# An adaLN block with linear attention and a routed softmax layer: the row statistics of the second modulated norm split over VectorE, ScalarE and GpSimd

## The chip, the cores and the metric
The kernel runs on 1 core of one Trainium2 chip. The metric is the device time of one execution in microseconds.

## The reference, cut to what matters
For each of 4 batches of 2048 rows with 256 elements the block computes:

```
h = layernorm(x) * (1 + ca) + sa
x = x + ga * favor_attention(h)              # linear attention, 16 heads
h = layernorm(x) * (1 + cb) + sb             # second modulation
x = x + gb * ffn(h)
ffn(h): for each of 4 experts (512 rows each)
    xn = (h - mean(h)) * rsqrt(var(h) + 1e-5) * norm_w + norm_b     # second statistics
    q, k, v = projections of the first 256 >> e elements of xn
  softmax attention over all 2048 rows, 8 heads
  out = projection + h
```

Every row of the second half thus needs two sets of statistics: those of x for the modulation, and those of the modulated row h for the norm inside the ffn. The change touches both.

## The kernel before, in words
The four batches run one after the other, each in three parts. The first part works over 16 tiles of 128 rows (linear attention features and sums). The last part is a long loop over 60 slots of score, exponential and value products (lines 1103, 1522, 893, 1695, 1707 and 1720). Between them lies a transition of some 80 us, and all edits are in it.

The transition goes over 4 slots s of 512 rows (one expert each, in the order 3, 1, 0, 2), each in two halves h of two 128-row tiles; I write (s, h). No planner decides anything: each engine has a list of calls written out by hand, and waits on semaphores. For one (s, h) the work is:

- TensorE: `projected` (L1571) puts out the attention output, `second_transposes` (L1580), `second_values` (L1590) and `second_qk` (L1600).
- VectorE: `residual` (L1146) adds to X; `statistics_of_x` (two L996, two L1000, one L1006) puts variance + eps in VE; `modulated` (two L1157, two L1161) makes Hh; `statistics_of_h` (two L996, two L1000, L1005, L1006) puts minus the mean in NEGM and variance + eps in VE; `merged` (L1139), `reciprocals` and `low_part` (L1171) serve other steps. `low_part` puts the low half of a q or k block in QKS.
- GpSimd: `deviations` (L564) takes VE to the power -0.5 for the modulation; `deviations_again` (L569, L571) does the same for the second statistics, and multiplies NEGM by it into NMR.
- ScalarE: `centred` (L773) makes X2 from Hh with scale RSTD and bias NMR; `normal` (L785), `second_values` (L791) and `high_part` (L802, the high half into QKS) empty TensorE's banks.
- SyncE: one in-order queue stores each block of QKS to q_scr or k_scr (L399) and, at the end of a slot, waits for the slot's stores and then loads operands for the last part (L378, L396, L410). Block n of q or k uses buffer n % 3 of QKS, so `high_part` of block n waits for the store of block n - 3. The blocks are 0 to 2 (slot 0), 3 to 5 (slot 1), 6 to 9 (slot 2) and 10 to 12 (slot 3).

GpSimd's calls for slot 2 stand in the order `deviations(2, 0)`, `deviations(2, 1)`, `deviations_again(2, 0)`, `deviations_again(2, 1)`.

## Time and profile before

| | us |
|---|---|
| median of 3 runs | 1781.54 |
| lowest and highest | 1776.65, 1785.52 |
| the profiled execution | 1779.44 |
| its span | 1777.6 |
| TensorE busy | 1692.4 (95%) |
| VectorE busy | 1381.0 (78%) |
| ScalarE busy | 1085.2 (61%) |
| GpSimd busy | 1123.3 (63%) |

The profiled execution took 1779.44 us, 1.8 us more than its span. Busy shares are means over parts with different limits; the transition is read by itself below. A matmul's end is modelled in the trace, so its start and the wait before it say more than its end. The granted clock of TensorE has a mean of 0.972 of full speed.

### The profile page before, as it was taken

The page shows a single profiled execution, that of the slowest core. Times are in us where ns is not written, and L with a number is a line of the kernel's source. Part 1 is how long each engine was busy: PE and PEld are TensorE (multiplying, and loading weights), DVE is VectorE, ACT ScalarE, POOL GpSimd, SP SyncE. Part 2 cuts the span into 40 slices and gives each one's busy share as a digit, 9 for nine tenths or more (in the row PEclk, how much of TensorE's full clock was granted, in tenths as well). Part 3 has the DMA queues.
Part 4 walks back from the last instruction along what each step waited for, and adds up shares of the span by engine and source line. Part 5 has one row for each costly group of instructions (what it writes and reads, how often), then busy time and mean ns, then how long its engine had stood idle before and what let it go on. Part 6 is the DMA issues. An engine that isn't in the chain of part 4 may idle for free.

```text
span 1777.6 us, 31990 instructions
## 1 busy us (share of the span) xinstructions
PE 1692.4 (95%) x11538; PEld 972.0 (55%) x11538; DVE 1381.0 (78%) x2629; ACT 1085.2 (61%) x2066; POOL 1123.3 (63%) x1058
## 2 busy tenths in 40 slices
PE   6999989999999989999999998999999999899998
PEld 4775544444577554444467755444437765444443
DVE  5987977776588788787678878877848878778783
ACT  1885536666688543666668844466667875356664
POOL 2784358677678344876767734686776862477774
PEclk8999989999999999999999999999999999899999
DMA  5000360010200045001110005400120001620201
GB/s 187 2 1 2 111 178 15 19 46 24 73 1 2 1 151 143 10 19 46 57 40 2 1 14 176 105 19 10 46 72 25 2 1 51 187 64 12 50 5 48
DMA packets 56077, 89.57 MB, mean 50 GB/s; under 512 B 13288, under 2 KB 31976, under 8 KB 53100
## 3 DMA queue, kind: packets, MB, share of 16 engines
q1 hardware_dynamic: 54768, 87.45, 17.0%
q8 instruction: 93, 1.52, 0.4%
q14 instruction: 64, 0.52, 0.1%
q10 hardware_dynamic: 1152, 0.07, 0.0%
HBM read 49.29 MB, written 35.72 MB: 48 GB/s over the span
## 4 chain that ended last, share of the span: by engine, by line
PE 69%; DVE 16%; ACT 8%; DMA 2%; issue 2%; SPq 2%; POOL 1%; ACTq 0%; DVEq 0%; POOLq 0%
PE PS L1695 14%; PE PS L1522 13%; PE PS L1707 12%; PE PS L1720 7%; PE PS L1416 5%; DVE MXP L1103 4%; PE PS L1441 3%; PE PS L1424 3%; PE PS L1451 3%; ACT HT L662 2%; ACT HTR L665 2%; DVE STAT L996 2%; DVE QKS L1171 1%; ACT PHIQ L703 1%; PE PS L1571 1%
## 5 line engine op out<-in xcount | busy, mean ns | idle before, releaser
L623 POOL TENSOR_TENSOR TS<-PR 128x1024 f32<-128x1024 f32 (+1 forms) x248 | 551.3, 2236 | 273.6 <-ACT PR L893 208.8
L1103 DVE TENSOR_REDUCE MXP<-PS 128x1 f32<-128x512 f32 x960 | 588.8, 681 | 145.2 <-PE PS L1522 144.6
L893 ACT ACTIVATE PR<-PS 128x512 f32<-128x512 f32 x960 | 487.5, 624 | 302.0 <-PE PS L1695 282.4
L1522 PE MATMUL PS<-KOP,QOP 96*128 96x512 f32 x960 | 406.2, 436 | 9.6 <-DVE MXP L1103 3.3
L1695 PE MATMUL PS<-QOP,KOP 97*128 97x512 f32 x960 | 389.7, 429 | 8.8 <-ACT PR L893 5.7
L1522 PEld LDWEIGHTS PS<-KOP,QOP 96*128 96x128 f32 x960 | 186.2, 195 | 168.9 <-issue 89.6
L1695 PEld LDWEIGHTS PS<-QOP,KOP 97*128 97x128 f32 x960 | 179.9, 189 | 153.1 <-ACT PR L893 130.1
L1707 PE MATMUL PS<-PR,V 128*32 128x512 f32 x1920 | 256.1, 607 | 0.0
L1707 PEld LDWEIGHTS PS<-PR,V 128*32 128x32 f32 x1920 | 65.8, 113 | 150.2 <-issue 110.8
L1720 PE MATMUL PS<-TS,ones 128*32 128x512 f32 x960 | 139.2, 618 | 0.0
L541 POOL TENSOR_SCALAR PK<-XSK 128x1024 f32<-128x1024 f32 x64 | 67.1, 1048 | 102.2 <-ACT XSK L725 102.2
L1451 PE MATMUL PS<-PB,QKT 64*128 64x256 f32 x1536 | 125.5, 296 | 1.0 <-DVE VE L990 1.0
L1451 PEld LDWEIGHTS PS<-PB,QKT 64*128 64x128 f32 x1536 | 99.3, 186 | 36.9 <-issue 25.4
L1416 PE MATMUL PS<-W1T,HTR 128*128 128x512 f32 x384 | 107.3, 415 | 2.7 <-POOL HTR L485 2.6
L501 POOL TENSOR_TENSOR SQ<-SQ 128x256 f32<-128x256 f32 (+2 forms) x192 | 96.1, 501 | 17.9 <-ACT SQ L682 3.1
L1043 DVE TENSOR_REDUCE MXQ<-PS 128x16 f32<-128x1024 f32 x64 | 78.3, 1223 | 21.2 <-PE PS L1451 21.1
L1441 PE MATMUL PS<-ident,XSQ 128*128 128x128 f32 x512 | 84.4, 292 | 9.5 <-ACT PHIQ L703 9.5
L494 POOL TENSOR_SCALAR XH<-X,MV,RSTD 128x256 f32<-128x256 f32 x64 | 78.4, 1225 | 11.0 <-POOL RSTD L478 10.4
L1053 DVE TENSOR_TENSOR XSK<-PS,MXK 128x1024 f32<-128x1024 f32 x64 | 78.4, 1225 | 7.1 <-DVE MXK L1049 0.9
L1043 DVE TENSOR_REDUCE MXK<-PS 128x16 f32<-128x1024 f32 x64 | 78.4, 1225 | 6.9 <-PE PS L1451 2.7
L703 ACT ACTIVATE PHIQ<-PS 128x512 f32<-128x512 f32 x128 | 76.3, 596 | 10.7 <-PE PS L1441 10.7
L564 POOL TENSOR_TENSOR RSTD<-VE,minus_half 128x2 f32<-128x2 f32 x32 | 22.9, 714 | 93.2 <-DVE VE L1006 93.2
(157 smaller groups left out, 2559.4 us busy)
## 6 DMA issues: line engine op xcount, KB each, us to landing
KOP<-k_scr SPq DMA_DIRECT2D x84, 256.0 KB, 5.6
k_scr<-QKS SPq DMA_DIRECT2D x64, 256.0 KB, 2.9
QOP<-q_scr SPq DMA_DIRECT2D x180, 64.0 KB, 2.0
q_scr<-QKS SPq DMA_DIRECT2D x40, 256.0 KB, 2.9
X<-in_L_attn_x_dram SPq DMA_DIRECT2D x16, 512.0 KB, 3.9
out_dram<-X SPq DMA_DIRECT2D x12, 512.0 KB, 2.9
QOP<-MXT SPq DMA_DIRECT2D x224, 0.5 KB
KOP<-QKS SPq DMA_DIRECT2D x36, 64.0 KB, 2.0
```

The lines of the kernel that those rows point to most:

```text
L501: g.tensor_tensor(sq[:, :, 0:w], sq[:, :, 0:w], sq[:, :, w:2 * w], ALU.add).then_inc(S["n2_half"], 1)
L623: g.tensor_tensor(sums(k)[:, 0:len(stage)], pair[:, :, 0], pair[:, :, 1], ALU.add).then_inc(S["psum_t"], 1)
L893: a.activation(PR[:, k % 2, w, q], bank(score_bank(p, n, w, q)), ACT.Exp).then_inc(S["ex"], 1)
L1043: return mark(v.tensor_reduce(mx[:], heads(src), AX.X, ALU.max))
L1103: v.tensor_reduce(MXP[:, u % 2, i, kc:kc + 1], bank(max_bank(p)), AX.X, ALU.max).then_inc(S["am_rd"], 1)
L1416: last = mm(bank(4), HTR[:, x_, k], W1T[:, w_, k], start=m == 0 and k == 0, stop=m == len(PARTS) - 1 and k == KD - 1)
L1441: last = tr(bank(at_bank)[:, q * P:(q + 1) * P], XSQ[:, t % 2, (half * 4 + q) * P:(half * 4 + q + 1) * P], ident[:])
L1451: last = mm(bank(base + r)[:, 2 * P * j:2 * P * (j + 1)], QKT[rows, x_, 2 * j + o], PB[rows, w_, j, 2 * P * r:2 * P * (r + 1)], start=m == ...
L1522: mm(bank(max_bank(p)), QOP[0:96, u % QS6, i * P:(i + 1) * P], KOP[0:96, h % KS6, kc * CH:(kc + 1) * CH], start=True, stop=True).then_inc( ...
L1695: mm(bank(score_bank(p, n, w, q)), KOP[:, units[u][0] % KS6, kt * P:(kt + 1) * P], QOP[:, u % QS6], start=True, stop=True).then_inc(S["sc_ ...
L1707: last = mm(PS[r:r + DH, 6, :], V2[:, 2 * n + q, h * DH:(h + 1) * DH], PR[:, k % 2, w, q], start=n == 0, stop=n == STEPS - 1, tile_positio ...
L1720: last = mm(PS[r:r + DH, 7, :], ones[:], sums(2 * m + q)[:, w], start=n == 0, stop=n == STEPS - 2, tile_position=(0, r))
```

## The change
The addition of eps to the variance of x moves from VectorE to GpSimd (`statistics` ends with L1000). `modulated`'s second instruction also puts out the row sum of h into NEGM (`accum_out`). GpSimd's new `means` scales that sum to minus the mean. ScalarE's new `squared` computes (h - mean)^2 for two tiles with the row sum into VE, and GpSimd's `deviations_again` scales that and adds eps before the power. `statistics_of_h` is gone from VectorE's list. The orders on ScalarE and GpSimd get the new calls.

```diff
                 def deviations(s, h):
-                    wait_all(pool, (S["ve2"], n))
+                    wait_all(pool, (S["ve2"], 2 * n))
+                    g.tensor_scalar(VE[:, cols], MV[:, cols, 1], NORM_EPS, None, ALU.add).then_inc(S["ve2_e"], 1)
+                    wait_all(pool, (S["ve2_e"], n))
                     g.tensor_tensor(RSTD[:, cols], VE[:, cols], minus_half[:, cols], ALU.pow).then_inc(S["rstd2"], 1)
+
+                def means(s, h):
+                    wait_all(pool, (S["h2"], 2 * n))
+                    g.tensor_scalar(NEGM[:, cols], NEGM[:, cols], -1.0 / D, None, ALU.mult).then_inc(S["negm"], 1)

                 def deviations_again(s, h):
                     wait_all(pool, (S["ve3"], 2 * n))
+                    g.tensor_scalar(VE[:, cols], VE[:, cols], 1.0 / D, NORM_EPS, ALU.mult, ALU.add
+                                    ).then_inc(S["ve3_e"], 1)
+                    wait_all(pool, (S["ve3_e"], n))
                     g.tensor_tensor(RSTD[:, cols], VE[:, cols], minus_half[:, cols], ALU.pow).then_inc(S["rs3"], 1)
-                    wait_all(pool, (S["rs3"], n))
+                    wait_all(pool, (S["rs3"], n), (S["negm"], n))
                     g.tensor_tensor(NMR[:, cols], NEGM[:, cols], RSTD[:, cols], ALU.mult).then_inc(S["nmr3"], 1)
...
                 deviations(2, 0)
+                means(2, 0)
+                deviations_again(2, 0)
                 deviations(2, 1)
-                deviations_again(2, 0)
+                means(2, 1)
                 deviations_again(2, 1)
...
+                def squared(s, h):
+                    act.wait_ge(S["negm"], 2 * (NC * b + s) + h + 1)
+                    for i in (2 * h, 2 * h + 1):
+                        t = s * TPC + i
+                        a.activation(XSQ[:, h, (i - 2 * h) * D:(i - 2 * h + 1) * D], Hh[:, t], ACT.Square,
+                                     bias=NEGM[:, t:t + 1], accum_out=VE[:, t:t + 1]).then_inc(S["ve3"], 1)
...
                 for t in tiles:
-                    v.bn_aggr(MV[:, t], STAT[:, t]).then_inc(S["dve_own"], 1)
-                    own.n += 1
-                dve.wait_ge(S["dve_own"], own.base + own.n)
-                sl = slice(tiles[0], tiles[-1] + 1)
-                if negated:
-                    v.tensor_scalar(NEGM[:, sl], MV[:, sl, 0], -1.0, None, ALU.mult).then_inc(S[signal], 1)
-                v.tensor_scalar(VE[:, sl], MV[:, sl, 1], NORM_EPS, None, ALU.add).then_inc(S[signal], 1)
+                    v.bn_aggr(MV[:, t], STAT[:, t]).then_inc(S[signal], 1)
...
                         v.scalar_tensor_tensor(Hh[:, t], Hh[:, t], RSTD[:, t:t + 1], MODB[:, b, 1, :], ALU.mult,
-                                               ALU.add).then_inc(S["h2"], 1)
-
-                def statistics_of_h(s, h):
-                    dve.wait_ge(S["h2"], TPC * (NC * b + s) + 2 * h + 2)
-                    statistics(halves(s, h), [Hh[:, t] for t in halves(s, h)], "ve3", negated=True)
+                                               ALU.add, accum_out=NEGM[:, t:t + 1]).then_inc(S["h2"], 1)
```

For the other slots GpSimd's list gets `means(s, h)` right ahead of `deviations_again(s, h)`. On ScalarE `squared(0, 0)` stands ahead of `centred(0, 0)`, `squared(0, 1)` behind it, `squared(1, 0)` ahead of `high_part(0, 0)`, `squared(1, 1)` ahead of `high_part(0, 1)`, `squared(2, 0)` ahead of `high_part(1, 0)`, `squared(2, 1)` ahead of `high_part(1, 1)`, `squared(3, 0)` ahead of `high_part(2, 0)` and `squared(3, 1)` ahead of `high_part(2, 3)`.

GpSimd's list for slot 2 in the kernel before (L564 is `deviations`, L569 and L571 `deviations_again`):

```order
L564 TENSOR_TENSOR RSTD<-VE,minus_half 128x2 [waits ve2] x2
L569 TENSOR_TENSOR RSTD<-VE,minus_half 128x2 [waits ve3]
L571 TENSOR_TENSOR NMR<-NEGM,RSTD 128x2 [waits rs3]
L569 TENSOR_TENSOR RSTD<-VE,minus_half 128x2 [waits ve3]
L571 TENSOR_TENSOR NMR<-NEGM,RSTD 128x2 [waits rs3]
```

The same place in the changed kernel, from `deviations(2, 0)` to `deviations(2, 1)` (L564 and L566 are `deviations` there, L571 is `means`, L576, L579 and L581 are `deviations_again`):

```order
L564 TENSOR_SCALAR VE<-MV 128x2 [waits ve2]
L566 TENSOR_TENSOR RSTD<-VE,minus_half 128x2 [waits ve2_e]
L571 TENSOR_SCALAR NEGM<-NEGM 128x2 [waits h2]
L576 TENSOR_SCALAR VE<-VE 128x2 [waits ve3]
L579 TENSOR_TENSOR RSTD<-VE,minus_half 128x2 [waits ve3_e]
L581 TENSOR_TENSOR NMR<-NEGM,RSTD 128x2 [waits negm,rs3]
L564 TENSOR_SCALAR VE<-MV 128x2 [waits ve2]
L566 TENSOR_TENSOR RSTD<-VE,minus_half 128x2 [waits ve2_e]
```

Both powers for the modulation stood together before; now four instructions for (2, 0) stand between them, and one of these waits for `ve3`, which ScalarE signals.

ScalarE's list from `second_values(1, 0)` to `high_part(1, 1)` in the kernel before:

```order
L791 ACTIVATE V2<-PS 128x512 [waits vp]
L802 ACTIVATE QKS<-PS,COLS 128x512 [waits scr0,qp]
L791 ACTIVATE V2<-PS 128x512 [waits vp]
L773 ACTIVATE X2<-Hh,NMR,RSTD 128x256 [waits x2T,nmr3]
L773 ACTIVATE X2<-Hh,NMR,RSTD 128x256
L802 ACTIVATE QKS<-PS,COLS 128x512 [waits scr1,qp]
```

And in the changed kernel (L788 is `squared`, L798 `centred`, L816 `second_values`, L827 `high_part`):

```order
L816 ACTIVATE V2<-PS 128x512 [waits vp]
L788 ACTIVATE XSQ,VE<-Hh,NEGM 128x256 [waits negm]
L788 ACTIVATE XSQ,VE<-Hh,NEGM 128x256
L827 ACTIVATE QKS<-PS,COLS 128x512 [waits scr0,qp]
L816 ACTIVATE V2<-PS 128x512 [waits vp]
L798 ACTIVATE X2<-Hh,NMR,RSTD 128x256 [waits x2T,nmr3]
L798 ACTIVATE X2<-Hh,NMR,RSTD 128x256
L788 ACTIVATE XSQ,VE<-Hh,NEGM 128x256 [waits negm]
L788 ACTIVATE XSQ,VE<-Hh,NEGM 128x256
L827 ACTIVATE QKS<-PS,COLS 128x512 [waits scr1,qp]
```

Two squares now stand ahead of each of the two `high_part` calls, and `squared(2, 1)` waits for `means(2, 1)`, which GpSimd's list has behind `deviations(2, 1)`.

## Rows read from the trace of the kernel before

**Rows 1.** The page: shares of the chain of work that ended last.
```profile
PE 69%; DVE 16%; ACT 8%; DMA 2%; issue 2%; SPq 2%; POOL 1%; ACTq 0%; DVEq 0%; POOLq 0%
```

**Rows 2.** The chain of waits, batch 1: start us, us, what.
```profile
646.19 0.66 DVE QKS L1171
646.87 0.32 SPq L399
...
656.80 2.84 DMA k_scr<-QKS
659.71 0.70 ACT QKS L802
```

**Rows 3.** Stretches: length, busy us PE, PEld, DVE, ACT, POOL; PEclk, DMA share, GB/s.
```profile
604.30:655.00 50.70, 49.52 (x249) 28.96 (x249) 48.47 (x155) 26.34 (x50) 14.09 (x25) 1.00 0.26 86
655.00:682.00 27.00, 22.00 (x62) 12.51 (x62) 19.27 (x33) 7.77 (x14) 13.29 (x14) 0.80 0.57 183
...
1471.20:1522.00 50.80, 49.59 (x250) 29.02 (x249) 48.56 (x155) 26.34 (x50) 14.14 (x25) 1.00 0.27 86
```

**Rows 4.** The same view, ten microseconds of batch 1.
```profile
616.00:626.00 10.00, 9.49 (x57) 5.34 (x57) 9.64 (x35) 6.92 (x14) 3.15 (x6) 1.00 0.02 7
```

**Rows 5.** TensorE's timeline: start us, us, what; in brackets idle before, releaser.
```profile
625.69 1.97 PE L1571 MATMUL PS<-WoG,MT 128*128 128x256 f32 x8 [0.51 <-DVE MT L1139]
...
661.33 0.66 PE L1580 MATMUL PS<-ident,X 128*128 128x128 f32 x2 [2.90 <-DVE QKS L1171]
```

**Rows 6.** Groups by line: line engine op xcount | busy us, mean ns | idle.
```profile
L1161 DVE SCALAR_TENSOR_TENSOR Hh<-Hh,RSTD,MODB 128x256 f32<-128x256 f32 x64 | 28.0, 478 | 0.0
...
L696 ACT ACTIVATE V<-PS 128x256 f32<-128x256 f32 x64 | 23.6, 369 | 0.0
...
L505 POOL TENSOR_TENSOR N<-SQ 128x32 f32<-128x32 f32 x64 | 16.0, 250 | 5.0
...
L1006 DVE TENSOR_SCALAR VE<-MV 128x2 f32<-128x2 f32 x64 | 10.6, 165 | 1.1
...
L571 POOL TENSOR_TENSOR NMR<-NEGM,RSTD 128x2 f32<-128x2 f32 x32 | 6.5, 204 | 2.5
...
L651 ACT ACTIVATE CE<-CT 128x8 f32<-128x8 f32 x1 | 0.2, 208 | 0.0
...
L473 POOL MEMSET COLM<- 128x4 f32 x1 | 0.1, 101 | 0.0
```

**Rows 7.** GpSimd's timeline, slot 2 of batch 1.
```profile
636.84 0.69 POOL L564 TENSOR_TENSOR RSTD<-VE,minus_half 128x2 f32<-128x2 f32 x1 [5.27 <-DVE VE L1006]
638.68 0.85 POOL L569 TENSOR_TENSOR RSTD<-VE,minus_half 128x2 f32<-128x2 f32 x1 [1.16 <-DVE VE L1006]
639.61 0.22 POOL L571 TENSOR_TENSOR NMR<-NEGM,RSTD 128x2 f32<-128x2 f32 x1
```

**Rows 8.** ScalarE's timeline, the same place.
```profile
635.66 0.60 ACT L791 ACTIVATE V<-PS 128x512 f32<-128x512 f32 x1 [0.37 <-PE PS L1590]
...
639.87 1.09 ACT L773 ACTIVATE X<-Hh,NMR,RSTD 128x256 f32<-128x256 f32 x2 [1.45 <-POOL NMR L571]
...
643.12 1.09 ACT L773 ACTIVATE X<-Hh,NMR,RSTD 128x256 f32<-128x256 f32 x2 [0.31 <-POOL NMR L571]
...
645.02 0.67 ACT L802 ACTIVATE QKS<-PS,QBS 128x512 fp32r<-128x512 f32 x1
```

**Rows 9.** VectorE's timeline, the same place.
```profile
637.30 0.74 DVE L996 BATCH_NORM_STATS2 STAT<-Hh 128x6 f32<-128x256 f32 x2
...
638.51 0.87 DVE L1157 SCALAR_TENSOR_TENSOR Hh<-X,MV,MODB 128x256 f32<-128x256 f32 x2
...
640.10 0.74 DVE L1171 SCALAR_TENSOR_TENSOR QKS<-PS,COLS,QKS 128x512 fp32r<-128x512 f32 x1
...
646.10 0.74 DVE L1171 SCALAR_TENSOR_TENSOR QKS<-PS,QBS,QKS 128x512 fp32r<-128x512 f32 x1
```

More of the change, by code:

```diff
@@ L223, in adaln_block @@
                    den den_sb num num_sb denT rec rb rT mt yps x1
-                   ve2 rs3 rstd2 ve3 nmr3 h2 x2 x2T xn_sb qp q_hi q_lo scr0 scr1 scr2 vp v2_sb vb_ok obm
+                   ve2 ve2_e rs3 rstd2 ve3 ve3_e negm nmr3 h2 x2 x2T xn_sb qp q_hi q_lo scr0 scr1 scr2 vp v2_sb vb_ok obm
                    q_in0 q_in1 q_in2 q_in3 q_in4 q_in5 kf0 kf1 kf2 kf3 k_in1 k_in2 k_in3 k_in4 k_in5 k_in6 k_in7
@@ L574, in batch @@
                 deviations(0, 1)
+                means(0, 0)
                 deviations_again(0, 0)
+                means(0, 1)
                 deviations_again(0, 1)
                 deviations(1, 0)
+                means(1, 0)
                 deviations_again(1, 0)
                 deviations(1, 1)
+                means(1, 1)
                 deviations_again(1, 1)
                 deviations(2, 0)
+                means(2, 0)
+                deviations_again(2, 0)
                 deviations(2, 1)
-                deviations_again(2, 0)
+                means(2, 1)
                 deviations_again(2, 1)
@@ L586, in batch @@
                 deviations(3, 1)
+                means(3, 0)
                 deviations_again(3, 0)
+                means(3, 1)
                 deviations_again(3, 1)
@@ L815, in batch @@
                 sums_out(2)
+                squared(0, 0)
                 centred(0, 0)
+                squared(0, 1)
+                normal(0, 0)
                 centred(0, 1)
-                normal(0, 0)
                 normal(0, 1)
@@ L823, in batch @@
                 spread(2, 1)
+                squared(1, 0)
                 high_part(0, 0)
@@ L828, in batch @@
                 second_values(0, 1)
+                squared(1, 1)
                 high_part(0, 1)
@@ L838, in batch @@
                 second_values(1, 0)
+                squared(2, 0)
                 high_part(1, 0)
@@ L841, in batch @@
                 centred(2, 0)
+                squared(2, 1)
                 high_part(1, 1)
@@ L846, in batch @@
                 normal(2, 1)
+                squared(3, 0)
                 high_part(2, 0)
@@ L851, in batch @@
                 high_part(2, 2)
+                squared(3, 1)
                 high_part(2, 3)
@@ L991, in third_set_up, with statistics @@
                 dve.wait_ge(S["setup_ok"], 1)
-            def statistics(tiles, srcs, signal, negated=False):
+            def statistics(tiles, srcs, signal):
                 for t, src in zip(tiles, srcs):
```

9 lines of the change are left out of this document (1 added, 8 removed).

## The prediction

> **What bounds the kernel now.** I read the chain first. TensorE has 69% of it and VectorE 16% [rows 1]. All edits are in the transitions, so I took the transition of batch 1 by itself, and compared one stretch with another batch: 604.30 to 655.00 us in batch 1 and 1471.20 to 1522.00 us in batch 3 agree within 0.1 us in every engine [rows 3]. One batch can be worked out and multiplied by 4.
>
> In that stretch VectorE is busy for 48.47 of 50.70 us, and the chain goes through it. That looks as if each microsecond taken off VectorE were a microsecond gained. But TensorE is busy for 49.52 of the same 50.70 us [rows 3]. The two are balanced. The one long wait of TensorE for VectorE in this part is 0.51 us, at 625.69 us [rows 5]. A relieved VectorE would wait for TensorE.
>
> Then comes the handover. VectorE's `low_part` of block 5 runs at 646.19 us in the chain. SyncE stores it from 646.87 us, loads, and gets block 6's store through by 656.80 + 2.84 = 659.64 us. ScalarE's `high_part` of block 9 starts at 659.71 us [rows 2]. TensorE has idled for 2.90 us when it goes on at 661.33 us [rows 5]. In this second stretch TensorE is busy for 22.00 of 27.00 us with a mean clock of 0.80 [rows 3]. So the number that decides a batch is **when block 5's low part is ready**: nothing behind it has slack, and work of TensorE just ahead of the wait has 2.9 us of it.
>
> **The change, part by part.**
>
> VectorE, per (s, h). Removed: two L996, two L1000, L1005 and L1006. In the timeline they take from 637.30 to 638.51 us, 1.21 us [rows 9]. L1006 of x goes too, about 0.1 us of a 0.165 us instruction. Added: two row sums that come out with L1161. The trace has none. The lower bound is nothing; the upper is a small VectorE instruction each, 0.165 us [rows 6]. I take 0.1 us, as small ones overlap. VectorE saves about 1.1 us per pair, 9 us per batch. By the two sections above this is worth at most the waits of TensorE for VectorE, 0.5 us, and the 0.4 us for which block 5's high part (ready at 645.02 + 0.67 = 645.69 us [rows 8]) waited for VectorE at 646.10 us [rows 9]: 0.9 us per batch if nothing else moved.
>
> ScalarE, per (s, h). Added: two squares of 128x256 with a row sum. The nearest row is the pair of L773 at this width, 1.09 us [rows 8]. The lower bound is two plain copies, 2 x 0.369 = 0.74 us; the upper one adds a small ScalarE instruction to each square for the sum, 1.09 + 2 x 0.208 = 1.51 us [rows 6, 8]. I take 1.15 us, near the row of the same shape. That makes 9 us per batch on an engine that is busy for 26.34 of 50.70 us [rows 3]. Its share is no trouble; its place is.
>
> GpSimd, per (s, h). Added: three instructions of 128x2. The nearest is L571 with 0.204 us; the bounds are 0.101 us (L473) and 0.250 us (L505) [rows 6]. With the hop over a semaphore I take 0.28 us each. Its total does not matter, its order does.
>
> **The path to block 5, step by step.** Before, `deviations(2, 1)` ran at 636.84 us, ahead of `deviations_again(2, 0)` [rows 7], and VectorE modulated (2, 1) at 638.51 us [rows 9]. Now it stands behind `deviations_again(2, 0)`, which waits for `squared(2, 0)`, and that stands behind the copy that ends at 635.66 + 0.60 = 636.26 us [rows 8]. From there:
>
> - TensorE's and ScalarE's delay from slots 0 and 1 (the squares stand there ahead of copies that TensorE waits for): 0.3 us, an estimate, since ScalarE has 3.08 us free of ten in the busiest stretch [rows 4] and two to three pairs of 1.15 us come into it. 636.55 us.
> - `squared(2, 0)`: 1.15 us. 637.7 us.
> - GpSimd's scale, power and product: 0.28 + 0.77 + 0.25 = 1.3 us, the power taken as 0.69 us [rows 7] and a hop. 639.0 us.
> - GpSimd's `deviations(2, 1)`: 0.28 + 0.77 = 1.05 us. 640.05 us, where VectorE used to begin at 638.51 us.
> - VectorE's modulation of (2, 1): 640.10 - 638.51 = 1.59 us before [rows 9], 0.2 us for the sums. 641.85 us.
> - GpSimd's `means`: 0.28 us. ScalarE's `squared(2, 1)`: 1.2 us with its hop. GpSimd: 1.3 us. 644.65 us, where `centred(2, 1)` began at 643.12 us before [rows 8].
> - `centred(2, 1)`, `normal(2, 0)`, `high_part` of block 5: as before 645.02 + 0.67 - 643.12 = 2.57 us [rows 8]. 647.25 us with a hop. VectorE is free now and starts at 647.35 us; before it was 646.10 us [rows 9].
>
> Block 5 comes **1.25 us later**. `squared(3, 0)` stands ahead of block 6's high part, but block 6 is needed only when SyncE has done its loads, so I cost that at nothing; its cover is what SyncE does from 646.87 us to 656.80 us [rows 2]. Late next, if it fails, is the store of block 6, one for one. The 0.3 us of slots 0 and 1 are in the sum already, and TensorE's delay ahead of block 9 hides in the 2.90 us.
>
> Sum: 4 x 1.25 = 5.0 us. Against the profiled execution of 1779.4 us that gives 1784.4 us; the median of the runs shown, 1781.5 us, is 2.1 us above that execution and gives 1786.5 us. I forecast **1785 us**. A measurement of this kernel can tell some 0.5%, 8.9 us, from no change.
>
> Bounds of the prices: the squares 2 x (-0.4 to +0.36) us, GpSimd's five new or moved small steps 5 x (-0.1 to +0.05) us, VectorE's sums -0.2 to +0.15 us, slots 0 and 1 from -0.5 to +1.0 us. Together per batch from -0.7 to +3.2 us, so 1777 to 1798 us.
>
> On the squares the Trainium skill (ScalarE: Activation LUTs, section "What ACT_TABLE_LOAD costs") states 280 ns + 0.833 ns per element for an ACTIVATE with a pointer bias and 93 ns of overlap, by which a pair would take an estimated 0.89 us and the sum would fall by 2 x 0.26 us per batch, to about 1783 us; it has no price for the sum, and the 1.09 us of the trace for two such instructions with one pointer more fits it.
>
> **The rivals.**
>
> *VectorE is the bound (faster).* The chain lies on VectorE from the first residual to block 5. Six pairs of statistics stand ahead of it, and 6 x 1.1 = 6.6 us per batch would go, 26 us in all: 1755 us. For it speaks the chain and 48.47 of 50.70 us. Against it speak TensorE's 49.52 of 50.70 us [rows 3], and that ScalarE and GpSimd now stand in the loop. It decides only if TensorE could run these steps closer together than it does. Chance 0.11, a part of it for smaller gains.
>
> *ScalarE becomes the bound in slots 0 and 1 (slower).* From 616 to 626 us ScalarE is busy for 6.92 us [rows 4]. Three pairs at 1.5 us make 11.4 us of ten: everything behind slips by 1.4 us, `sums_out(3)` and the copies among it, and TensorE, which has 1.2 us free in 50.7, does not make it up. Per batch 1.25 + 1.4 + 2 x 0.35 for the dearer squares on the path = 3.35 us, 13.4 us in all: 1793 to 1795 us. It decides from about 1.05 us per pair if all three pairs fall into that stretch, and not at all if one of them slips out. Chance 0.26.
>
> *The summing form of the modulation runs at half rate (a little slower).* L1161 reads two 256-element rows from SBUF in 0.478 us [rows 6], and the trace has no such instruction with a sum. At half rate the elements' part, which I take as 0.27 of the 0.478 us, would double, 0.54 us per pair. Once per batch that lies on the path: 4 x 0.54 = 2.2 us, 1787 us. Chance 0.08. The Trainium skill (Vector Engine (DVE) Microarchitecture Reference, section "Points that are easy to get wrong") says that this shape with two non-bf16 SBUF sources halves throughput since no port is left for reading back the accumulator. Without a sum the trace speaks against a halving: 0.478 us is like other instructions of this length.
>
> *The forecast:* chance 0.55.
>
> **How the numbers follow.** Faster by over 0.5% comes from the first rival: 0.11. Slower by over 0.5% takes 2.2 us per batch or more: most of the second rival (0.22) and the upper part of the bounds of the forecast (0.05), 0.27. The rest, 0.62, is within 0.5%. The range of 8 in 10 takes in the bounds of the prices and the second rival, and leaves out most of the first: 1768 to 1799 us.
>
> **What would show it.** In the changed profile: VectorE's busy time falls by 30 to 40 us and its share from 604 to 655 us to about 0.8; the pair of squares takes 1.0 to 1.3 us; GpSimd's power for (2, 1) begins about 2.5 us later than 636.84 us against the same start of the transition; block 5's low part begins 1 to 1.5 us later; the waits of TensorE from 604 to 655 us are for ScalarE and not for VectorE; and the stretch behind block 5 keeps its length. I am wrong if block 5 comes earlier than before, if a pair of squares takes over 1.5 us, or if the loop of the last part changes its pace.

## The result and the profile after

The changed kernel takes **1788.89 us** (median of 17 runs, 1784.82 to 1791.79), the kernel before 1779.57 us (median of 17, 1775.85 to 1785.52): a ratio of 1.005, 95% interval 1.0041 to 1.0059. That is 9.3 us, about 0.5%, slower. The profiled execution took 1791.79 us with a span of 1790.0 us, against 1779.44 and 1777.6 us before.

The page of the changed kernel: its span, busy time by engine, and the chain of work that ended last:

```profile
span 1790.0 us, 32086 instructions
...
PE 1697.2 (95%) x11538; PEld 973.4 (54%) x11538; DVE 1343.8 (75%) x2469; ACT 1115.7 (62%) x2194; POOL 1143.7 (64%) x1154
...
PE 67%; ACT 11%; DVE 9%; POOL 5%; issue 4%; DMA 2%; SPq 1%; ACTq 0%; POOLq 0%; DVEq 0%
```

VectorE was relieved as meant, by 37.2 us; ScalarE got 30.5 us and GpSimd 20.4 us. On the chain VectorE falls from 16% to 9%, and ScalarE, GpSimd and plain issue rise from 11% to 20% [rows 1]. This has to be split by place. In the four transitions alone the chain has 150 us of VectorE before and 38 us after, 84 and 150 us of TensorE, 6 and 48 us of ScalarE, none and 14 us of GpSimd: there the work has become a relay of small steps between engines. Most of GpSimd's 5%, 63 us, lies elsewhere: in the loop of the third batch the chain runs along GpSimd's sums (L641) instead of TensorE. The pace is the same there; 94 us of that loop, the kernel before first, then the changed one:

```profile
1170.07:1264.07 94.00, 94.00 (x554) 45.22 (x554) 73.96 (x132) 58.64 (x116) 67.56 (x30) 1.00 0.12 31
1172.70:1266.70 94.00, 94.00 (x554) 45.00 (x554) 74.34 (x132) 59.34 (x117) 68.03 (x31) 1.00 0.13 31
```

The groups of the new instructions, by line and form:

```profile
L1188 DVE SCALAR_TENSOR_TENSOR Hh<-Hh,RSTD,MODB 128x256 f32<-128x256 f32 x64 | 28.4, 480 | 0.0
L1184 DVE SCALAR_TENSOR_TENSOR Hh<-X,MV,MODB 128x256 f32<-128x256 f32 x64 | 28.0, 478 | 16.4 <-POOL RSTD L566 16.4
...
L788 ACT ACTIVATE XSQ<-Hh,NEGM 128x256 f32<-128x256 f32 x64 | 31.8, 499 | 22.9 <-POOL NEGM L571 22.9
...
L788 ACT ACTIVATION_READ_ACCUMULATOR XSQ<-Hh,NEGM 128x1 f32 x64 | 12.1, 189 | 0.0
...
L571 POOL TENSOR_SCALAR NEGM<-NEGM 128x2 f32<-128x2 f32 x32 | 7.8, 242 | 38.5 <-DVE Hh L1188 38.5
L564 POOL TENSOR_SCALAR VE<-MV 128x2 f32<-128x2 f32 x32 | 7.7, 240 | 54.3 <-DVE MV L1033 53.0
...
L576 POOL TENSOR_SCALAR VE<-VE 128x2 f32<-128x2 f32 x32 | 6.1, 191 | 67.2 <-ACT XSQ L788 67.2
L1188 DVE DVE_READ_ACCUMULATOR Hh<-Hh,RSTD,MODB 128x1 f32 x64 | 5.3, 83 | 0.0
```

A sum that comes out of an instruction is an instruction more in the trace. VectorE's is 83 ns long but runs beside the next instruction: the modulation of two tiles holds VectorE for 1.61 us (641.48 to 643.09 us), where it was 1.59 us before [rows 9]. ScalarE's is 189 ns long, and about half of it overlaps. The summing modulation takes 480 ns where the plain one took 478 [rows 6].

Batch 1 of the changed kernel starts at 598.32 us (the memset of MXN, L1124), that of the kernel before at 596.51 us (L1097). So I take 1.81 us off when I compare. The two stretches of [rows 3] and the one of [rows 4], shifted by 1.81 us:

```profile
606.11:656.81 50.70, 48.57 (x246) 28.47 (x247) 39.92 (x116) 33.25 (x81) 17.13 (x45) 1.00 0.26 85
656.81:683.81 27.00, 21.04 (x64) 11.87 (x63) 17.70 (x30) 8.35 (x17) 15.13 (x17) 0.87 0.58 185
...
617.81:627.81 10.00, 9.47 (x57) 5.16 (x56) 7.07 (x21) 8.45 (x23) 4.25 (x11) 1.00 0.02 8
```

VectorE's share of the first stretch fell from 48.47 to 39.92 us, and TensorE is busy for 0.95 us **less** of it. In the ten microseconds of slots 0 and 1 ScalarE is busy for 8.45 us, and TensorE for 9.47 us, as before. The time is lost in slot 2: block 2's low part still comes 0.4 us earlier than before. GpSimd's timeline there:

```profile
639.10 0.19 POOL L576 TENSOR_SCALAR VE<-VE 128x2 f32<-128x2 f32 x1 [3.68 <-ACT XSQ L788]
639.37 0.71 POOL L579 TENSOR_TENSOR RSTD<-VE,minus_half 128x2 f32<-128x2 f32 x1
640.16 0.19 POOL L581 TENSOR_TENSOR NMR<-NEGM,RSTD 128x2 f32<-128x2 f32 x1
640.43 0.22 POOL L564 TENSOR_SCALAR VE<-MV 128x2 f32<-128x2 f32 x1
640.74 0.70 POOL L566 TENSOR_TENSOR RSTD<-VE,minus_half 128x2 f32<-128x2 f32 x1
643.26 0.22 POOL L571 TENSOR_SCALAR NEGM<-NEGM 128x2 f32<-128x2 f32 x1 [1.81 <-DVE Hh L1188]
```

VectorE's timeline:

```profile
641.48 0.88 DVE L1184 SCALAR_TENSOR_TENSOR Hh<-X,MV,MODB 128x256 f32<-128x256 f32 x2 [2.56 <-POOL RSTD L566]
...
643.09 0.75 DVE L1194 SCALAR_TENSOR_TENSOR QKS<-PS,COLS,QKS 128x512 fp32r<-128x512 f32 x1
...
648.58 0.75 DVE L1194 SCALAR_TENSOR_TENSOR QKS<-PS,QBS,QKS 128x512 fp32r<-128x512 f32 x1 [0.76 <-ACT QKS L827]
```

ScalarE's timeline:

```profile
637.94 0.50 ACT L788 ACTIVATE XSQ<-Hh,NEGM 128x256 f32<-128x256 f32 x1
638.34 0.19 ACT L788 ACTIVATION_READ_ACCUMULATOR XSQ<-Hh,NEGM 128x1 f32 x1
638.43 0.50 ACT L788 ACTIVATE XSQ<-Hh,NEGM 128x256 f32<-128x256 f32 x1
638.83 0.19 ACT L788 ACTIVATION_READ_ACCUMULATOR XSQ<-Hh,NEGM 128x1 f32 x1
...
645.97 1.09 ACT L798 ACTIVATE X<-Hh,NMR,RSTD 128x256 f32<-128x256 f32 x2 [0.80 <-POOL NMR L581]
```

Block 5's low part now starts at 648.58 us; before it was 646.10 us [rows 9], 647.91 us with the shift: 0.67 us later, against 1.25 us predicted. VectorE had been idle for 2.56 us ahead of the modulation and for 0.76 us ahead of block 5. TensorE's waits:

```profile
647.12 0.66 PE L1595 MATMUL PS<-ident,X 128*128 128x128 f32 x4 [0.94 <-ACT X L798]
...
663.71 0.66 PE L1595 MATMUL PS<-ident,X 128*128 128x128 f32 x2 [3.66 <-DVE QKS L1194]
```

The wait for VectorE of 0.51 us at 625.69 us [rows 5] is gone; one for `centred` of 0.94 us has come, and the wait ahead of block 9 has grown from 2.90 to 3.66 us.

**Where the 12.4 us between the two spans are.** I split each execution at two marks per batch: the start of the transition (the memset of MXN) and its top (ScalarE's first QOP row, L880 or L913). The half-clock time of a stretch is 2 x (1 - granted clock) x length, from the trace's clock records without rounding; it is the time at 1.2 GHz instead of 2.4. (A clock of two digits, as the views print it, is too coarse for this: 0.005 of 1303 us is 13 us of half clock.) Here for all kernels of this study:

```
kernel (profiled execution)   4 transitions   4 last parts   half clock of     last parts less half
                                   us              us          these, us       of their half clock
before                            314.0           1302.9           62                1272.0
after                             317.7           1310.6           76                1272.8
e1_order                          318.0           1307.5           68                1273.4
e2_x_eps                          310.3           1298.0           51                1272.5
e3_less_vector                    309.6           1304.0           65                1271.4
e4_h_only                         315.6           1305.4           69                1271.0
e5_block5                         308.6           1304.1           58                1275.1
e7_x_eps_block5                   307.5           1299.6           52                1273.6
e8_after_block5                   316.0           1302.1           59                1272.8
e9_narrow_squares                 314.4           1302.7           59                1273.4
e10_fewer_small                   312.5           1308.1           80                1268.4
e11_after_filled                  319.6           1306.5           72                1270.7
e12_before_filled                 312.6           1301.2           52                1275.2
e13_e7_filled                     304.1           1310.1           76                1272.3
```

The transitions took 3.7 us more, the start of the program 1.1 us (it takes 160.0 to 161.8 us in these kernels, and nothing in it was changed), and the last parts (with the next batch's first part) 7.7 us. No work of the last parts was changed. If TensorE alone set their pace, a microsecond of half clock would cost half a microsecond, and the 13.6 us more of it would explain 6.8 of the 7.7 us. Less half of their half-clock time the four stretches take 1268 to 1275 us in every kernel here, where they take 1298 to 1311 us as they are. The remaining spread of 7 us is too wide to settle a difference of 7.7 us by itself, so here are the last parts one by one, those of the first three batches of all 14 executions:

```
half clock of one last part, us    how many    its length, us
7                                   1          352.9
10                                  4          352.4 to 353.0
13 to 14                           12          354.2 to 355.9
17                                  6          354.4 to 355.2
20 to 21                           17          356.5 to 357.6
27                                  2          359.3 to 359.4
```

Changed kernels and kernels like the one before stand mixed in these groups; a last part's length goes with its half-clock time, whichever kernel it belongs to, at 0.37 us per microsecond by a straight line through the 42. So 5 us (by that line) to 6.8 us (by the half) of the 7.7 us are the lower clock. The stretches at 1.2 GHz come at the same places in all kernels, some 3 to 6, 193 to 199, 209 to 218 and 348 to 353 us behind the top; they differ in how long they last, and now and then one is missing. The 40 us with the second and the third of these places in the third batch, the kernel before first:

```profile
1300.00:1340.00 40.00, 38.69 (x214) 17.20 (x214) 15.07 (x31) 23.31 (x47) 29.94 (x20) 0.96 0.25 80
```

And of the changed kernel:

```profile
1300.00:1340.00 40.00, 38.57 (x187) 14.59 (x180) 12.98 (x28) 20.58 (x41) 27.42 (x16) 0.83 0.25 79
```

The work of the two is shifted by up to 4 us against each other. TensorE is as busy, with fewer instructions (187 for 214), at a granted clock of 0.83 for 0.96. One execution is one draw of this. Over the runs, the mean granted clock was 0.9692 in the changed kernel's 17 and 0.9745 in 23 of the kernel before, so the lower clock is not an accident of one execution.

### The profile page after: what moved, and what is told of

It is laid out like the page before. It is cut to its first block, busy times and chain, and to the rows that moved or that the text cites. A ratio compares the mean times of both kernels' runs of the same rounds, so it can differ in the third digit from the quotient of the medians.

```text
span 1790.0 us, 32086 instructions
## 1 busy us (share of the span) xinstructions
PE 1697.2 (95%) x11538; PEld 973.4 (54%) x11538; DVE 1343.8 (75%) x2469; ACT 1115.7 (62%) x2194; POOL 1143.7 (64%) x1154
## 4 chain that ended last, share of the span: by engine, by line
PE 67%; ACT 11%; DVE 9%; POOL 5%; issue 4%; DMA 2%; SPq 1%; ACTq 0%; POOLq 0%; DVEq 0%
PE PS L1710 12%; PE PS L1537 11%; PE PS L1722 11%; PE PS L1735 6%; PE PS L1431 5%; DVE MXP L1130 4%; POOL TS L641 4%; PE PS L1456 4%; PE PS L1439 3%; PE PS L1466 3%; ACT HT L680 2%; PE PS L1586 2%; ACT HTR L683 2%; ACT PHIQ L721 1%; PE PS L1556 1%
## 5 line engine op out<-in xcount | busy, mean ns | idle before, releaser
L641 POOL TENSOR_TENSOR TS<-PR 128x1024 f32<-128x1024 f32 (+1 forms) x248 | 551.2, 2235 | 276.6 <-ACT PR L926 218.9
L1722 PE MATMUL PS<-PR,V 128*32 128x512 f32 x1920 | 260.1, 615 | 0.0
L494 POOL TENSOR_SCALAR XH<-X,MV,RSTD 128x256 f32<-128x256 f32 x64 | 78.5, 1227 | 11.0 <-POOL RSTD L478 10.4
L1431 PEld LDWEIGHTS PS<-W1T,HTR 128*128 128x128 f32 x384 | 67.9, 190 | 23.8 <-POOL HTR L485 4.9
```

The source lines that it names most:

```text
L641: g.tensor_tensor(sums(k)[:, 0:len(stage)], pair[:, :, 0], pair[:, :, 1], ALU.add).then_inc(S["psum_t"], 1)
L1431: last = mm(bank(4), HTR[:, x_, k], W1T[:, w_, k], start=m == 0 and k == 0, stop=m == len(PARTS) - 1 and k == KD - 1)
L1722: last = mm(PS[r:r + DH, 6, :], V2[:, 2 * n + q, h * DH:(h + 1) * DH], PR[:, k % 2, w, q], start=n == 0, stop=n == STEPS - 1, tile_positio ...
```

## The experiments

All with 6 to 12 runs, on three chips; the ratios are to the kernel before on the same chip, whose medians there are 1778.9, 1779.5 and 1779.3 us. "Block 5" below is the start of its low part after the start of the transition: 49.57 to 49.60 us in the kernel before, 50.25 to 50.28 us in the changed one.

**Is GpSimd's order the cause?** The changed kernel with the order of slot 2 as it was:

```diff
                 deviations(2, 0)
-                means(2, 0)
-                deviations_again(2, 0)
                 deviations(2, 1)
+                means(2, 0)
+                deviations_again(2, 0)
                 means(2, 1)
```

> The change, with GpSimd's list for slot 2 in the old order: deviations(2, 1) stands ahead of means(2, 0) and deviations_again(2, 0). In the changed profile VectorE began to modulate (2, 1) 43.2 us after the transition's start (its memset of MXN), before the change 42.0 us; block 5's low part began at 50.26 us, before 49.59 us. Theory A (the wait behind deviations_again delays block 5): VectorE begins at about 41 us, block 5's low part at 49.0 us or earlier, and the kernel gains 4 x 0.6 to 4 x 1.3 us on the changed kernel, ratio to the kernel before about 1.002 or less. Rival B (ScalarE's squares ahead of high_part and centred alone delay it): VectorE begins early, but block 5 stays at 50.0 us or later and the time stays with that of the changed kernel, ratio 1.004 to 1.006.

Measured: 1786.6 us (1783.36 to 1792.62), ratio 1.0047 (1.0031 to 1.0063). VectorE modulates (2, 1) 2 us earlier, and block 5 stays at 50.26 to 50.43 us. GpSimd's timeline in this run:

```profile
638.62 0.22 POOL L564 TENSOR_SCALAR VE<-MV 128x2 f32<-128x2 f32 x1 [5.04 <-DVE MV L1033]
638.92 0.71 POOL L566 TENSOR_TENSOR RSTD<-VE,minus_half 128x2 f32<-128x2 f32 x1
639.71 0.52 POOL L571 TENSOR_SCALAR NEGM<-NEGM 128x2 f32<-128x2 f32 x1
```

And ScalarE's:

```profile
640.26 0.51 ACT L788 ACTIVATE XSQ<-Hh,NEGM 128x256 f32<-128x256 f32 x1 [2.03 <-POOL NEGM L571]
...
642.71 1.09 ACT L798 ACTIVATE X<-Hh,NMR,RSTD 128x256 f32<-128x256 f32 x2 [0.31 <-POOL NMR L581]
643.71 0.49 ACT L788 ACTIVATE XSQ<-Hh,NEGM 128x256 f32<-128x256 f32 x1
...
646.16 1.09 ACT L798 ACTIVATE X<-Hh,NMR,RSTD 128x256 f32<-128x256 f32 x2 [0.80 <-POOL NMR L581]
```

The in-order queue blocks at its other end. `means(2, 0)` now stands behind `deviations(2, 1)`, which waits until 638.62 us for VectorE's statistics. So ScalarE waits for 2.03 us with `squared(2, 0)`, and `squared(2, 1)` comes behind `centred(2, 0)`. What was won for one half is lost on the other. The order is no cause by itself. The third order, `means(2, 0)` first, then `deviations(2, 1)`, then `deviations_again(2, 0)`, would avoid both waits by the times of these two traces, and make the scale of (2, 0) wait for the power of (2, 1) instead; it was not tried.

**Which part of the change costs?** Only the epsilon of x's variance on GpSimd, all else as before (below is GpSimd's part of the edit; VectorE's statistics of x end with the aggregation, as in the change):

```diff
-                    wait_all(pool, (S["ve2"], n))
+                    wait_all(pool, (S["ve2"], 2 * n))
+                    g.tensor_scalar(VE[:, cols], MV[:, cols, 1], NORM_EPS, None, ALU.add).then_inc(S["ve2_e"], 1)
+                    wait_all(pool, (S["ve2_e"], n))
                     g.tensor_tensor(RSTD[:, cols], VE[:, cols], minus_half[:, cols], ALU.pow).then_inc(S["rstd2"], 1)
...
```

> The kernel before, with one part of the change: only the addition of eps to the variance of x moves from VectorE (0.165 us) to GpSimd (0.223 us), statistics of h stay on VectorE. If TensorE and the statistics of h set the pace, nothing is seen: block 5's low part within 0.2 us of 49.59 us after the start, ratio 0.999 to 1.001. If each microsecond of VectorE counts, 6 pairs x 0.1 us come off: 49.0 us, 2.4 us less in all, ratio 0.9985.

Measured: **1771.69 us** (1769.69 to 1776.22), ratio 0.9966 (0.9952 to 0.9979). Block 5 at 48.47 to 48.63 us, 1.0 to 1.1 us earlier; the transitions take 310.3 us instead of 314.0. The small part of the change is good by itself. It brought more to block 5 than both expectations, since the instruction was worth more than the 0.1 us that they took for it: a pair's statistics of x hold VectorE for 1.14 to 1.17 us in the kernel before (635.53 to 636.70 us, for one) and for 0.94 to 1.00 us here, since the wait for the aggregation, ahead of it, went too. The start of one such pair here, and the instruction behind it:

```profile
630.95 0.74 DVE L998 BATCH_NORM_STATS2 STAT<-X 128x6 f32<-128x256 f32 x2
...
631.89 0.66 DVE L1145 TENSOR_TENSOR MT<-PS,NUMS 128x512 f32<-128x512 f32 x1
```

Of the 7.2 us by which the medians differ, 3.7 us are in the transitions; the last parts of the profiled execution are 4.9 us shorter, with 51 us of half clock instead of 62.

The other part only, h's statistics over three engines with x's epsilon on VectorE:

> The change without its other part: the statistics of h go as in the change, the addition of eps to the variance of x stays on VectorE. One step less of 0.223 us and a hop of 0.08 us on GpSimd on the path to (2, 1), another VectorE step that fits into its idle time. Theory: block 5's low part at about 49.95 us after the start against 50.26 us of the change, and 4 x 0.3 = 1.2 us less than the change, ratio to the kernel before 1.002 to 1.005. Rival (GpSimd's small steps aren't on the path): 50.26 us, the time of the change.

Measured: 1781.08 us (1778.6 to 1786.97), ratio 1.0016 (1.0006 to 1.0027), block 5 at 49.78 to 49.85 us, transitions 315.6 us. So h's part costs 1.6 us in the transitions; x's part takes 3.7 us off them when it is made alone, and adds 2.1 us when it is made on top of h's. The parts do not add up, and the sign of one depends on the other. In the kernel before VectorE is busy for 48.47 of 50.70 us [rows 3], and an instruction off it pays as far as TensorE has room. In the changed kernel VectorE idles ahead of the modulation and waits for GpSimd, where the moved instruction now stands in series.

**What is relief of VectorE worth?** The kernel before without the two L996 of h's statistics; the second statistics are then of old values, all else is done:

> The kernel before without the two bn_stats of h per pair (the second statistics are then aggregated from those of x, so that part of the computation is left out); nothing is added anywhere. VectorE has 8 x 0.74 us less in each transition, some 4.5 us of it ahead of block 5. The theory of the prediction (TensorE is as full as VectorE, so relief is worth at most 0.9 us per batch): block 5's low part at 48.6 to 49.3 us after the start, against 49.59 us, and 1 to 4 us less in all, ratio 0.998 to 0.9995. The rival (VectorE is the bound): block 5 at 45 us, 4 x 4.5 = 18 us less, ratio 0.990.

Measured: 1775.66 us (1763.73 to 1778.41), ratio 0.9971 (0.9955 to 0.9986); block 5 at 48.36 to 48.43 us. The stretch that answers to the first of [rows 3]:

```profile
600.08:650.78 50.70, 50.58 (x259) 30.66 (x259) 44.27 (x140) 26.37 (x50) 16.59 (x28) 1.00 0.27 89
```

VectorE has 4.2 us less to do in it, and TensorE is busy for 50.58 of 50.70 us. Some 1.2 us came out of it, and no more can: TensorE is full.

**ScalarE's squares or GpSimd's small steps?** The changed kernel with narrow squares:

```diff
-                        a.activation(XSQ[:, h, (i - 2 * h) * D:(i - 2 * h + 1) * D], Hh[:, t], ACT.Square,
+                        a.activation(XSQ[:, h, (i - 2 * h) * D:(i - 2 * h) * D + 32], Hh[:, t, 0:32], ACT.Square,
```

> The changed kernel with its squares taken over the first 32 of 256 elements; the sum of squares is then not that of the row, and nothing else is left out. A square of 497 ns should take about 0.31 us, so that a pair costs about 0.4 us less of ScalarE, and 8 pairs 3 us per batch. Theory S (ScalarE's added time on the path of slot 2 is what delays block 5): two or three pairs lie on the path, block 5's low part comes 0.7 to 1.1 us earlier, 49.2 to 49.5 us, and the time falls by 3 to 5 us to 1784. Rival G (the GpSimd steps and hops between the engines are what delays it): block 5 comes less than 0.4 us earlier, and the time stays within 2 us of the changed kernel's 1788.

Measured: 1780.19 us (1774.36 to 1783.45), ratio 0.9999 (0.9988 to 1.001). A square takes 313 ns, and its read of the accumulator still 190 ns:

```profile
L788 ACT ACTIVATE XSQ<-Hh,NEGM 128x32 f32<-128x32 f32 x64 | 19.8, 313 | 22.6 <-POOL NEGM L571 22.6
...
L788 ACT ACTIVATION_READ_ACCUMULATOR XSQ<-Hh,NEGM 128x1 f32 x64 | 12.2, 190 | 0.0
```

Block 5 comes at 49.14 to 49.15 us, 1.1 us earlier, the transitions take 314.4 us, 3.3 us less than in the changed kernel. The converse, the changed kernel with two of GpSimd's three small steps left out (lines 564 and 576):

> The changed kernel without GpSimd's addition of epsilon to x's variance and without its scale and epsilon on the sum of squares; both powers take the sums as they are, so the normalisation is off by a constant, and only these two small steps per pair are left out. Theory G (GpSimd's new small steps stand in series on the path to block 5): one such step of x for (2,1) at 0.30 us with its hop and two of h at 0.23 us lie on it, and block 5's low part comes 0.6 to 0.8 us earlier than 50.25 us, 49.5 us, the time falls by 3 us or more. Rival S (only ScalarE's squares count): less than 0.3 us earlier.

Measured: 1781.47 us (1772.15 to 1784.13), ratio 1.0005 (0.9991 to 1.0018); block 5 at 49.25 to 49.30 us, 1.0 us earlier, and the transitions at 312.5 us, 5.2 us less. Each theory had named its own engine alone; both engines are on the path. The narrow squares took 0.37 us off each pair, two or three of which count, 0.7 to 1.1 us. The left-out steps took some 0.85 us off the path of (2, 1): 0.31 us from start to start for line 564 and 0.27 us twice for line 576. The gain of 1.1 and 1.0 us is thus at least one for one; a part of it arises already in slots 0 and 1, where block 2's low part comes 0.7 and 0.4 us earlier. In slot 2 modulation, `means`, square, scale, power, product and `centred` follow one another, and each waits for the one before it. Of the 8.7 and 7.4 us by which these two kernels are faster than the changed one, only 3.3 and 5.2 us are in the transitions.

**Does block 5 decide the batch?** The kernel before with block 5's parts ahead of other calls:

```diff
                 high_part(1, 1)
+                high_part(1, 2)
                 centred(2, 1)
                 normal(2, 0)
-                high_part(1, 2)
                 normal(2, 1)
...
                 statistics_of_x(3, 0)
-                statistics_of_x(3, 1)
                 low_part(1, 2)
+                statistics_of_x(3, 1)
```

> The kernel before, with block 5's high part moved on ScalarE ahead of centred(2,1) and normal(2,0), and its low part on VectorE moved ahead of statistics_of_x(3,1). No work is added or taken away. Theory P (block 5's low part decides the batch through the store, the loads and block 9's high part): block 5's low part falls from 49.6 us after the start of the transition to about 47 us, and the top of the transition from 78.5 us to about 76.5 us; 4 x 2 = 8 us, about 1771 us against a kernel before at 1779. Rival Q (the DMA's own queue, or block 6's low part, decides from there on): block 5 comes at 47 us, and the top stays at 78.2 to 78.7 us; within 2 us of the kernel before.

Measured: 1775.91 us (1769.68 to 1781.15), ratio 0.9971 (0.9959 to 0.9984). Block 5 at 48.42 to 48.44 us (1.15 us earlier, not the 2.6 us expected: ScalarE waits for TensorE's block), transitions 308.6 us, 1.3 us less each. The low part of block 9 comes 0.9 us earlier; the rest of the 1.3 us goes with TensorE's clock, which is lower for 14 us of these transitions instead of 24. The same edit in the changed kernel:

> The changed kernel, with the same move of block 5's two parts as in e5_block5, and nothing else. In the changed kernel block 5's high part stands behind squared(2,1), centred(2,1) and normal(2,0); centred(2,1) waits for the squares and GpSimd. Theory P: block 5's low part goes from 50.25 us to 47 or 48 us, past the centred wait, and the top from 79.4 us to about 77 us: 8 to 10 us, 1779 us or a little less, so the change costs nothing that this move does not give back. Rival C (most of the change's cost is a lower granted clock that comes from elsewhere): the top falls, but the time stays above 1784 us with a granted clock of 0.967 to 0.969 in the whole span.

Measured: 1781.81 us (1777.68 to 1786.45), ratio 1.0008 (0.9999 to 1.0016). Block 5 at 48.49 to 48.50 us, 1.76 us earlier, but the transitions take 316.0 us, only 0.4 us less each. The chain of waits shows what stands there instead:

```profile
639.23 0.68 DVE QKS L1194
639.92 0.57 SPq L396
...
643.91 0.56 SPq L399
644.47 0.04 issue
644.52 3.49 DMA q_scr<-QKS
648.07 0.32 SPq L378
```

SyncE's queue is busy from 639.92 us with the copies into KOP (L396) and then the stores of blocks 3 and 4; the store of block 5 goes out only behind them, and has landed at 648.01 us. In the changed kernel its two issues began at 649.35 us and the loads at 652.58 us, 3.23 us later (below, with the start of the loads); here it is 4.16 us, from 643.91 us to 648.07 us. So 0.9 us of the 1.76 us go into the longer store, and 0.3 us into the wait for the queue (block 5's low part starts 1.03 us ahead of its issue, where it was 0.77 us):

```profile
649.35 0.80 SPq L399 DMA_DIRECT2D q_scr<-QKS  x2
652.58 4.03 SPq L378 DMA_DIRECT2D QOP<-q_scr  x9
```

So block 5 decides the batch when it is late, about one for one, and hardly once it is so early that it meets the stores of blocks 3 and 4 in SyncE's queue: block 9's low part follows block 5 by 0.3 us for 0.2 in e4_h_only, 0.8 for 0.7 in the changed kernel, and, the other way, 1.0 for 1.0 in e2_x_eps and 1.2 for 1.2 in e3_less_vector, but only 0.4 for 1.76 here. Of the 7.1 us by which this kernel is faster than the changed one, 1.7 us are in the transitions of the profiled executions; the last parts are 8.5 us shorter, with 59 us of half clock instead of 76.

**The lower clock.** TensorE idles for 3.66 us ahead of block 9, and the granted clock of the 13 us behind it is 0.74, a mixture of both levels; in the kernel before it is 0.74 too, behind 2.90 us. I filled the wait with work that leaves the results as they are: the values of (2, 1) computed two and a half times.

```diff
-                    for i in range(2):
+                    for i in (1, 0, 1, 0, 1)[0 if (s, h) == (2, 1) else 3:]:
```

> The changed kernel, with TensorE kept busy in its wait ahead of block 9: it computes the values of (2,1) two and a half times, 12 more matmuls of 128x256 into the same place, 2.8 us of the 3.66 us that it idles for there. ScalarE reads these values only 4.9 us after they are ready now, so nothing on the path is later. Theory K (part of the change's cost is a lower granted clock that follows TensorE's idle time in the transition): the stretch from 64 to 77 us after the transition's start shows more than 0.74 to 0.76, the sum of half-clock time falls from 117 to 100 us or less, the top of the transition comes earlier, and the time falls by 5 us or more, to 1784 or less. Rival (the clock does not depend on this idle time, or the longer path alone makes the time): clock and time stay, 1787 to 1790.

> The kernel before, with the same 12 more matmuls in its wait of 2.90 us ahead of block 9. Theory K: the same gain or a smaller one, since before starts from 99 us of half clock: 1774 to 1777 us, and then the difference between the changed kernel and the one before shrinks from 9 us towards the 3.7 us by which the transitions are longer. Rival: 1778 to 1780 us, and the difference stays at 9 us.

Measured: changed and filled 1785.98 us (1779.29 to 1793.3), ratio 1.0041 (1.0026 to 1.0056); before and filled 1778.76 us (1771.85 to 1782.82), ratio 0.9999 (0.9987 to 1.0011). The 13 us that begin 64 us after the start of the transition in batch 1, first in the changed kernel:

```profile
662.32:675.32 13.00, 10.99 (x27) 6.38 (x27) 8.86 (x15) 5.73 (x11) 9.41 (x10) 0.74 0.42 145
```

In the changed kernel with the wait filled:

```profile
660.08:673.08 13.00, 9.06 (x30) 4.95 (x28) 9.10 (x15) 6.10 (x11) 9.46 (x10) 1.00 0.49 166
```

The clock of the stretch came back to 1.00, so its fall does follow TensorE's idle time. But the transitions did not get shorter: 319.6 us in the changed kernel filled against 317.7 us, 312.6 us in the kernel before filled against 314.0 us. It would be wrong to take the lower clock for free, though. These 13 us hold a part of the wait ahead of block 9, and that ends later here. From block 9's low part to the top the work is the same, 37 matmuls, and starts at one event. Batch 1, first the changed kernel, then the same filled:

```profile
662.81:677.48 14.67, 12.99 (x37) 7.34 (x37) 10.98 (x19) 5.38 (x10) 8.92 (x10) 0.77 0.45 147
```

```profile
661.39:674.91 13.52, 10.42 (x37) 5.73 (x37) 10.89 (x19) 5.39 (x11) 8.23 (x8) 1.00 0.49 156
```

The stretch is 1.15 us shorter at full clock. TensorE's work got 2.57 us shorter, and more than half of that went into waits, one of 1.64 us for operands that SyncE loads among them. All 56 transitions of this study agree: in the 11 without any half clock behind block 9 the stretch takes 13.45 to 13.53 us, in 42 others it takes 14.06 to 14.70 us, and in the remaining three 15.15 to 16.16 us. Two of the 11 are of kernels without the filling (e5_block5 and e7_x_eps_block5, batch 2, 13.47 us each), so it is the clock and not the filling that shortens it. The lower clock thus costs a transition about 1.1 us.

Two things ate that gain here. In the changed kernel filled only one of the four transitions was free of half clock behind block 9. And block 9's low part came later, by 2.1 us over the four batches there and by 2.9 us in the kernel before filled, behind a store of block 6 that landed later; in the first batch it was on time, and in the fastest kernel filled (below) it was not later over the four. Whether the filling delays it is not shown.

The half-clock time of the last parts fell from 76 to 72 us in the changed kernel and from 62 to 52 us in the kernel before; over the runs the mean granted clock rose from 0.9692 to 0.9735 and from 0.9746 to 0.9796. In the changed kernel the sum over the whole execution fell from 117 to 96 us, as far as theory K asked, but the time fell by 2.9 us instead of 5 and more, and the intervals of the two ratios overlap. What sets the half-clock time of the last parts stays open.

**A version that beats both.** x's epsilon on GpSimd and block 5's parts ahead, in the kernel before:

> The kernel before, with two edits at once: the epsilon of x's statistics on GpSimd (that alone brought 1.1 us to block 5 in each batch and a ratio of 0.9966), and block 5's two parts moved ahead as in the run e5_block5. Theory P: the gains on block 5 add, low part at about 46 us and top at about 75.5 us, 4 x 3 = 12 us, 1766 to 1768 us. Rival Q: it is the epsilon run's time again, 1772 us, since block 6's part decides.

Measured: **1769.35 us** (1765.49 to 1776.07), ratio 0.9942 (0.9924 to 0.996), the fastest here; block 5 at 47.49 us. With TensorE's wait filled as well:

> The fastest kernel so far (the kernel before with x's epsilon on GpSimd and block 5's parts moved ahead, 1769.35 us, ratio 0.9942), with the values of (2,1) computed twice, 8 more matmuls, 1.9 us of the 2.3 to 3.2 us that TensorE idles for ahead of block 9. Theory K: fewer half-clock microseconds than its 82 us and 1764 to 1767 us. Rival: 1768 to 1771 us.

Measured: 1773.49 us (1766.47 to 1779.69), ratio 0.9966 (0.995 to 0.9983). It has the shortest transitions of all, 304.1 us, without any half clock in them: 3.4 us less than the version without the filling, nearly all of it behind block 9. It gives that back in its last parts, 1310.1 us with 76 us of half clock instead of 1299.6 us with 52. Both are single profiled executions; the intervals of the ratios overlap, and no gain in time is shown for the filling.

## Why the prediction was right or wrong

The time, 1788.9 us, lay in the range and on the side of the forecast's mechanism; 1785 us was 3.9 us short. As a change it was further off: the forecast started from a median of 1781.5 us over 3 runs, which is 1779.6 us over 17, so that 3.5 to 5 us were forecast and 9.3 us came. Point by point:

- **TensorE is as full as VectorE, so the relief brings next to nothing.** Right. 37 us came off VectorE, within the 30 to 40 us; the run without L996 shows what such relief brings alone, 1.2 us per batch, where I had bounded it at 0.9 us. What I mispriced is L1006 of x: 0.1 us was taken for it, and it is 0.2 us per pair with its wait, so that x's epsilon alone brought 1.0 to 1.1 us to block 5.
- **The prices.** The pair of squares 1.08 us (637.94 to 638.83 + 0.19 us), against 1.15 us; GpSimd's small steps 0.19 to 0.24 us and 0.27 to 0.31 us from start to start, against 0.28 us; VectorE's two sums 0.02 us more on the engine against 0.2 us, since their 83 ns overlap (from the modulation to `means` it was 1.78 us all the same, as the hop to GpSimd took the place of the sums); the modulation not at half rate. Right, but for the sums. The Trainium skill (Vector Engine (DVE) Microarchitecture Reference, section "Points that are easy to get wrong") has it that such a shape with two non-bf16 SBUF sources loses half its throughput to the accumulator; these rows, 480 ns against 478 ns, do not show it.
- **The path to block 5.** The steps came in the order given. On the clock of the kernel before, `squared(2, 0)` began at 637.94 - 1.81 = 636.13 us where I had 636.55; the modulation of (2, 1) at 639.67 where I had 640.05; `centred(2, 1)` at 644.16 where I had 644.65; block 5 at 646.77 where I had 647.35. **The step that was mis-sized is "TensorE's and ScalarE's delay from slots 0 and 1: 0.3 us".** There was none: `second_values(1, 0)` began at 637.44 - 1.81 = 635.63 us where it was 635.66 us before, `squared(2, 0)` overlapped its end by 0.1 us, and block 2's low part came at 36.71 us after the start instead of 37.15. That is 0.4 us of the 0.58; the rest is the squares and `centred`. The path gave 0.67 us per batch instead of 1.25, below the 1 to 1.5 us that the prediction named as its sign, and GpSimd's power for (2, 1) began 2.1 us later instead of 2.5.
- **"The order of GpSimd" as its reason.** It was the path that was followed, but not a cause: with the order restored block 5 stays where it was. The forecast held because both orders cost the same.
- **"Nothing behind it has slack", one for one.** Right in the direction of the change: 4 x 0.67 = 2.7 us at block 5, 3.2 us at block 9, 3.7 us at the top. In the other direction it holds for the first microsecond (e2_x_eps, e3_less_vector); block 5 earlier by 1.76 us in the changed kernel brought 0.4.
- **The sum.** Transitions 3.7 us against 5.0 us. Of the 12.4 us between the two spans 7.7 us are in the last parts, 5 to 6.8 us of them by the lower granted clock, of which the sum had no term, and 1.1 us ahead of the first transition, where nothing was changed. "The loop of the last part changes its pace" was named as a sign of error, and it did: by the clock, with the same work. That the number came near is in part luck: a path that was too long, and a cost that was not seen. The upper end of the range of prices, 1798 us, adds 4 x 3.2 us to the forecast, which holds 4 x 1.25 us of it already; from the kernel before it would be 1792 to 1794 us.
- **ScalarE as the bound in slots 0 and 1.** It did not come: 8.45 us of ten, and block 2 was early. **VectorE as the bound**: no. **The summing form at half rate**: no.

## What to carry to other kernels

Before work is taken off a busy engine, look whether another is as full beside it; then only the order and the latency of the path count, and each hop to a third engine is paid in full. Split such a change and try its parts alone: here the small part took 3.7 us off the transitions by itself and added 2.1 us together with the rest. And where kernels differ by half a percent, compare the stretch that was changed by itself, and set the length of the unchanged stretches beside their granted clock: the place where a saving is made and the place where it shows are not the same.

## What the runs showed that I had not expected

- A row sum on ScalarE is an ACTIVATION_READ_ACCUMULATOR of 189 ns, at 256 elements as at 32 (190 ns), half of it overlapped: a square with its sum takes 0.49 us from start to start. On VectorE it is one of 83 ns that the next instruction covers: two sums made the modulation of a pair 0.02 us longer.
- A VectorE instruction of 165 ns that has to wait for the one before it was worth 0.20 us when it was taken away.
- At full clock the same 37 matmuls at the end of a transition took 10.4 us instead of 13.0 us, but the stretch, which also waits for loads, became only 1.1 us shorter.
- The half-clock time of the last parts went from 51 to 80 us between kernels whose last parts are the same, and their length from 1298 to 1311 us; the six kernels with h's statistics on three engines and the wait unfilled had a mean clock of 0.9692 to 0.9716 over their runs, the five without (the kernel before among them) 0.9728 to 0.9748. What links the two is not settled.
